# Layer 1's routing: experts chosen from logits in two parts, ranks summed by TensorE into one bank, two-byte columns with the tile innermost, gather ids first

## The reference, cut to what matters

```
logits = xf @ Wg                                  # (4096, 8)
probs = softmax(logits, axis=-1)
vals, idx = top_k(probs, 2)
w = vals / (sum(vals, axis=-1, keepdims=True) + 1e-09)
counts = zeros(8); combine = zeros((4096, 8))
for k in range(2):
    oh = one_hot(idx[:, k], 8)
    pos = cumsum(oh, axis=0) - 1 + counts[None, :]    # rank in the expert's queue
    keep = (oh == 1) & (pos < 256)
    counts = counts + sum(keep, axis=0)
    combine = combine + w[:, k][:, None] * keep
out = sum over e of combine[:, e] * (gelu(xf @ W1[e] + b1[e]) @ W2[e] + b2[e])
```

## Time and profile before

| | us |
|---|---|
| median of 3 runs | 897.94 |
| lowest, highest | 897.37, 899.93 |
| the profiled execution, its own time | 897.85 |
| the profiled execution, its span | 895.6 |

### The profile page before, as it was taken

One profiled execution on the slowest core, in us unless ns is written; L12 is line 12 of the kernel. 1 busy time (PEld: TensorE's weight loads), 2 busy tenths in 40 slices (PEclk: granted clock), 3 DMA queues, 4 the chain that ended last, 5 costly groups with the idle time before them and its releaser, 6 DMA issues.

```text
span 895.6 us, 33689 instructions
## 1 busy us (share of the span) xinstructions
PE 713.8 (80%) x14638; PEld 644.2 (72%) x14639; DVE 658.0 (73%) x1076; ACT 491.7 (55%) x724; POOL 558.3 (62%) x412
## 2 busy tenths in 40 slices
PE   4467636882688999999999999999999988915846
PEld 2137425771677999899989899988988887904846
DVE  3788553453587999999999999999998989284104
ACT  5465302342474677578668667757676656554310
POOL 4011046524257989988999988888878888404630
PEclk9677658996699999999999999999999999855978
DMA  7731142331006000000000000000000000420137
GB/s 192 242 79 48 49 90 58 71 64 54 21 5 193 6 10 7 6 7 10 7 6 10 18 4 4 15 4 3 4 15 4 4 15 16 149 100 26 46 105 200
DMA packets 67595, 44.01 MB, mean 49 GB/s; under 512 B 22000, under 2 KB 62208, under 8 KB 67328
## 3 DMA queue, kind: packets, MB, share of 16 engines
q1 hardware_dynamic: 64128, 35.11, 13.8%
q0 software_dynamic: 3328, 6.82, 3.3%
HBM read 27.76 MB, written 14.16 MB: 47 GB/s over the span
## 4 chain that ended last, share of the span: by engine, by line
PE 67%; DVE 10%; issue 9%; ACT 7%; another core or an unknown queue 3%; DMA 2%; SPq 2%; POOL 1%; DVEq 0%; POOLq 0%; ACTq 0%
PE psum L1811 16%; PE psum L1911 6%; PE psum L1866 6%; PE psum L1844 6%; PE psum L1902 4%; PE psum L1873 3%; PE psum L1859 3%; PE psum L1881 3%; PE psum L1745 2%; ACT arena L1007 2%; PE psum L2120 2%; PE psum L1760 2%; PE psum L1852 2%; PE psum L1620 1%
## 5 line engine op out<-in xcount | busy, mean ns | idle before, releaser
L1811 PE MATMUL psum<-hT,w_qkv 128*128 128x128 f32 x1408 | 173.9, 281 | 2.0 <-DVE arena L1363 1.6
L1811 PEld LDWEIGHTS psum<-hT,w_qkv 128*128 128x128 f32 x1408 | 164.5, 194 | 5.2 <-DVE arena L1363 1.8
L563 POOL TENSOR_TENSOR arena<-arena,small 128x1024 f32<-128x1024 f32 x56 | 106.0, 1914 | 56.1 <-DVE small L1376 56.1
L542 POOL TENSOR_TENSOR arena<-arena 128x1024 f32<-128x1024 f32 x56 | 106.7, 1905 | 12.6 <-ACT arena L890 11.4
L528 POOL TENSOR_TENSOR arena<-arena 128x1024 f32<-128x1024 f32 x56 | 106.5, 1902 | 0.0
L1369 DVE TENSOR_REDUCE small<-arena 128x16 f32<-128x1024 f32 x60 | 73.1, 1219 | 8.8 <-ACT arena L879 6.6
L518 POOL DMA_INDIRECT arena<-h_rows,route x40 | 40.2, 1004 | 58.1 <-issue 43.2
L567 POOL TENSOR_TENSOR arena<-arena 128x1024 f32<-128x1024 f32 x28 | 65.9, 2353 | 16.3 <-DVE arena L1396 16.2
L1357 DVE TENSOR_REDUCE small<-psum 128x16 f32<-128x1024 f32 x60 | 72.8, 1215 | 2.6 <-PE psum L1911 2.6
L1363 DVE TENSOR_TENSOR arena<-psum,small 128x1024 f32<-128x1024 f32 x60 | 70.5, 1215 | 0.1
L1844 PE MATMUL psum<-arena 64*128 64x64 f32 x1344 | 62.4, 231 | 10.0 <-issue 7.4
(11 more groups left out here) (319 smaller groups left out, 1643.7 us busy)
## 6 DMA issues: line engine op xcount, KB each, us to landing
y_rows<-hT SPq DMA_DIRECT2D x8, 512.0 KB, 6.6
arena<-y_rows SPq DMA_DIRECT2D x8, 512.0 KB, 6.0
o_rows<-arena SPq DMA_DIRECT2D x10, 256.0 KB
x_sb<-in_L_attn_u SPq DMA_DIRECT2D x8, 256.0 KB, 4.6
arena<-in_W_inT SPq DMA_DIRECT2D x16, 128.0 KB
arena<-in_W_out SPq DMA_DIRECT2D x64, 32.0 KB
h_rows<-arena SPq DMA_DIRECT2D x4, 512.0 KB, 3.3
h_rows<-hT SPq DMA_DIRECT2D x8, 256.0 KB, 2.3
```

What stands on the lines that cost most here:

```text
L542: pool.tensor_tensor(x3, x3, lr[:, tile_of(t) * 32 + k * H:tile_of(t) * 32 + k * H + H].unsqueeze(2).to_broadcast([P, H, D]), ALU.mult).th ...
L563: pool.tensor_tensor(z4, z4, r3.unsqueeze(3).to_broadcast([P, 8, 2, CH]), ALU.mult).then_inc(done, 1)
L1811: mm = pe.matmul(ps[bank][:, p * P:(p + 1) * P], w_qkv[:, j * HD + p * P:j * HD + (p + 1) * P], hT[:, at:at + P], start=True, stop=True)
```

## The change

All of it lies in steps 1 to 7 above.

- The logits of chunks 0 to 5 get a signal of their own. PE now does the logits of chunks 4 and 5 before it turns chunk 6, those of chunk 6 before it turns chunk 7. The second part goes to another bank. Tiles are numbered chunk by chunk.
- DVE chooses the experts by the logits minus their maximum, read straight from PSUM, in eleven operations: once for chunks 0 to 5 (192 elements) and once for chunks 6 and 7 (64). One-hot columns are written as bf16 with expert and choice outermost and the tile innermost. After each part it adds up the columns from chunk to chunk (`sum_up`, eight operations of 64 elements).
- ACT's exponential stands aside from the choice; a second small one gives the second value relative to the first, and the weights come from these.
- PE forms complete ranks in one bank: columns ahead in the tile, running sums of the chunk before, and full sums of the batch pairs before (in the line with `all_ones` and the one with `first_half`), besides the expert totals in four matmuls of 8 columns.
- DVE multiplies, caps, adds and reduces that to the rank, in five operations; the two products of number and slot half are between bf16 operands with the tile innermost.
- The gather's ids are made in five operations right after PE's result; the scatter's follow.
- POOL makes one more mask and one more table at the start.

```diff
+        masks = sb("masks", [P, 5 * P], BF16)
+        pair_no = sb("pair_no", [P, 2 * T], BF16)
...
+            chain.link(pool.memset(first_half[CH:P, :], 0.0))
+            chain.link(pool.memset(first_half[0:CH, 0:CH], 0.0))
+            chain.link(pool.iota(pair_no[:, :], pattern=[[T, 2], [1, NC], [NC, BP]], base=1, channel_multiplier=0, **imprecise))
...
-            act.activation(pr1, sh1, ACT.Exp).then_inc(ex_done, 1)
+            act.activation(pr1, sh1, ACT.Exp)
+            act.activation(tile_f, tile_f, ACT.Exp).then_inc(ex_done, 1)
...
+            def choose(lg, c0, c1):
+                ...
+                chain.link(dve.tensor_reduce(per(mx), part(lg), AX_X, ALU.max))
+                chain.link(dve.tensor_tensor(part(sh1), part(lg), wide(mx), ALU.subtract))
+                chain.link(dve.scalar_tensor_tensor(part(pick1), part(sh1), 0.0, order, ALU.is_equal, ALU.mult))
+                chain.link(dve.tensor_reduce(per(m2), part(pick1), AX_X, ALU.max))
+                chain.link(dve.tensor_tensor(hot(0), part(pick1), wide(m2), ALU.is_equal))
+                chain.link(dve.scalar_tensor_tensor(part(sh2), hot(0), -1e30, part(sh1), ALU.mult, ALU.add))
+                chain.link(dve.tensor_reduce(per(tile_f), part(sh2), AX_X, ALU.max))
+                chain.link(dve.tensor_tensor(part(sh2), part(sh2), wide(tile_f), ALU.is_equal))
+                chain.link(dve.tensor_tensor(part(sh2), part(sh2), order, ALU.mult))
+                chain.link(dve.tensor_reduce(per(m2), part(sh2), AX_X, ALU.max))
+                return dve.tensor_tensor(hot(1), part(sh2), wide(m2), ALU.is_equal)
...
+            dve.wait_ge(lg_mm, 2)
+            chain.link(choose(ps[1][:, L:L + T * E], 0, NC - 2))
+            for c in range(NC - 3):
+                chain.link(sum_up(c))
+            sum_up(NC - 3).then_inc(rhs_ready, 1)
+            dve.wait_ge(rhs_ready, 3)
+            dve.wait_ge(lg_mm, 3)
+            choose(ps[0][:, 0:T * E], NC - 2, NC).then_inc(oh_done, 1)
+            dve.wait_ge(oh_done, 2)
+            chain.link(sum_up(NC - 2))
+            sum_up(NC - 1).then_inc(rhs_ready, 1)
+            dve.tensor_tensor(et(numbers[:, 0:512]), et(oh1), over_e2(pair_no[:, :], E), ALU.mult)
+            chain.link(dve.tensor_scalar(numbers[:, 512:1024], oh1, part_no, None, ALU.mult))
             dve.wait_ge(ex_done, 2)
             chain.link(dve.tensor_reduce(e_sum, te(pr1), AX_X, ALU.add))
+            chain.link(dve.scalar_tensor_tensor(row_f, e_sum, 1e-9, tile_f, ALU.mult, ALU.add))
+            chain.link(dve.tensor_scalar(row_f, row_f, 1.0, None, ALU.add))
+            chain.link(dve.reciprocal(wk[:, 0:T], row_f))
+            dve.tensor_tensor(wk[:, T:2 * T], wk[:, 0:T], tile_f, ALU.mult).then_inc(wk_set, 1)
             dve.wait_ge(cnt_done, 2)
+            dve.tensor_tensor(k3(scr1)[:, :, 0, :], k3(ranks)[:, :, 0, :], k3(oh1)[:, :, 0, :], ALU.mult)
+            chain.link(dve.tensor_scalar(cap1, total, float(CAP), None, ALU.min))
+            chain.link(dve.tensor_tensor(r3, k3(ranks)[:, :, 1, :], cap1.unsqueeze(2).to_broadcast([P, E, T]), ALU.add))
+            chain.link(dve.tensor_tensor(k3(scr1)[:, :, 1, :], r3, k3(oh1)[:, :, 1, :], ALU.mult))
+            chain.link(dve.tensor_reduce(pos, scr1.rearrange("p (e t) -> p t e", e=E), AX_X, ALU.add))
+            dve.tensor_scalar(first, pos, float(P), None, ALU.is_lt)
+            chain.link(dve.tensor_scalar(beyond, pos, float(P), None, ALU.is_ge))
+            dve.scalar_tensor_tensor(rows_b[:, :], beyond, -float(P), pos, ALU.mult, ALU.add)
+            chain.link(dve.scalar_tensor_tensor(second, pos, float(CAP), beyond, ALU.is_lt, ALU.mult))
+            for j, tile in enumerate((first, second)):
+                last = dve.tensor_tensor(r4[:, j], numbers..., over_e2(tile, 2 * E), ALU.mult)
...
+            chain.link(dve.tensor_copy(in3, found[:, :, E:2 * E]))
+            chain.link(dve.scalar_tensor_tensor(row3, found[:, :, 0:E], float(P), in3, ALU.mult, ALU.add))
             chain.link(dve.tensor_scalar(in3, row3, -float(P), 0.0, ALU.add, ALU.max))
             chain.link(dve.tensor_scalar(off3, in3, float(B * L), -float(B * L), ALU.is_ge, ALU.mult))
+            dve.tensor_tensor(ids_i[:, 0:2 * E]..., in3, off3, ALU.add).then_inc(ids_set, 1)
...
-            for c in range(3, NC):
+            for c in range(3, NC - 2):
                 second_turn(c)
                 second_logits(c - 2)
+            second_logits(NC - 4)
+            second_logits(NC - 3).then_inc(lg_mm, 1)
+            second_turn(NC - 2)
             second_logits(NC - 2)
+            second_turn(NC - 1)
             second_logits(NC - 1).then_inc(lg_mm, 1)
...
+            def ahead_in_tile(c0, c1):
+                pe.matmul(tiles_of(ranks, c0, c1), before_own, tiles_of(oh1, c0, c1), start=(c0 == 0), stop=False)
+            def ahead_in_batch(c0, c1):
+                pe.matmul(tiles_of(ranks, c0, c1), own_ones, tiles_of(up_to, c0 - 1, c1 - 1), start=False, stop=False)
             pe.wait_ge(rhs_ready, 3)
+            ahead_in_tile(0, NC - 2)
+            ahead_in_batch(1, NC - 2)
             pe.wait_ge(rhs_ready, 4)
+            ahead_in_tile(NC - 2, NC)
+            ahead_in_batch(NC - 2, NC)
+            for b in range(BP - 1):
+                pe.matmul(r4[:, :, :, b + 1:BP], all_ones, sums[:, :, b:b + 1].unsqueeze(2).to_broadcast([P, 2 * E, NC, BP - 1 - b]),
+                          start=False, stop=False)
+            pe.matmul(r4, first_half, sums.unsqueeze(2).to_broadcast([P, 2 * E, NC, BP]), start=False, stop=True)
+            for b in range(BP):
+                mm = pe.matmul(ps[2][:, 512:512 + E], all_ones, first_sums[:, :, b], start=(b == 0), stop=(b == BP - 1))
+            mm.then_inc(cnt_done, 1)
+            pe.wait_ge(rhs_ready, 5)
...
-                mm = pe.matmul(ps[0][:, 0:32], hot_of(pos_hot, t), rhs1[:, t * 32:(t + 1) * 32],
+                mm = pe.matmul(ps[0][:, 0:32], hot_of(pos_hot, t), rhs1.rearrange("p (r t) -> p r t", t=2 * T)[:, :, t],
```

More of the change, by code:

```diff
@@ L1508, in _ @@
-            dve.tensor_copy(ohb1, oh1).then_inc(rhs_ready, 1)
-            chain.link(dve.tensor_tensor(row_f, top[0], top[1], ALU.add))
-            chain.link(dve.tensor_scalar(row_f, row_f, 1e-9, None, ALU.add))
-            chain.link(dve.reciprocal(row_f, row_f))
-            for k in range(2):
-                last = dve.tensor_tensor(wk[:, k * T:(k + 1) * T], top[k], row_f, ALU.mult)
-            last.then_inc(wk_set, 1)
-            dve.wait_ge(cnt_done, 2)
-            own, both, pref = ps[3][:, 512:1024], ps[2][:, 0:512], ps[3][:, 0:512]
@@ L1556, in _ @@
             last.then_inc(rhs_ready, 1)
-            chain.link(dve.tensor_copy(rows_b[:, :], row1))
             for n in range(2 * T // 8):
```

121 lines of the change are left out of this document (41 added, 80 removed).

## The result

| | before | changed |
|---|---|---|
| median of 20 runs each, us | 902.98 | 894.68 |
| lowest, highest | 896.90, 908.24 | 889.97, 901.11 |
| the profiled execution, its own time | 897.85 | 894.4 |
| its span | 895.6 | 892.6 |

The ratio is 0.9904 [0.9881, 0.9926]: faster, but by 8.3 us where 12.2 were forecast (0.9864).

A forecast was written before the change was run, and what follows sets the result against it. The prediction took the serial routing, 30.9 us of small DVE operations from 784.50 to 815.36, as the bound. Its terms brought the ids to 803.15, a gain of 12.2: 897.85 - 12.2 = 885.7 us, range 883.0 to 889.0.

The forecast's parts named there:

- Logits in two parts: PE's logits ahead of routing: second signal at 786.4 against 784.50, a price of 1.9 us for two bare ACT copies.
- Choice, part one: DVE's choice over 192 elements, from 779.7 to 785.5 beside PE, ending 0.9 before the second logits.
- Ranks and numbers: PE's rank matmuls give counts at 791.45; DVE's numbers 0.33 + 0.30, weights signalled 791.9; later two one-hot products, 1.25 together.
- Ids: DVE's five operations of 16 ahead of the gather: 1.05 us, ids at 803.15 where before 815.36.
- The diagonal matrices: ACT's 64 matrices, needed by the first expert product's end at 813.1, end at 810.7: cover 2.4, where it was 12.3.
- the constants: POOL's wider mask, two memsets and table at the start: some 0.85, hidden beside PE's DMA wait until 9.31, so nothing.
- A: Narrow PSUM runs slow the rank matmuls: at four times the column price 887.1, with dearer number products 887.9; chance 0.10.
- B: Scattered reads of 32 columns make PE the bound of the id stage: at twice the pitch 890.5; chance 0.07.
- E: Slower: the id matmuls' scattered reads so dear that the gain is lost, 901.4 at 10 ns a column; chance 0.04.
- C: ACT's diagonal matrices become the bound and gelu waits: 887.8 at a slip of 4.5; chance 0.03.
- D: Expert stage falls into another rhythm; PE's 2.34 idle ahead of the seventh expert vanishes or recurs: 883.3 or 888; chance 0.06.
- The rule on memory lines: Weighed against PE's new operands: access to other 16-byte SBUF lines costs, non-contiguous PSUM access slows matmuls; no figure given.

The follow-up runs named there:

- delay: Changed kernel with six additional DVE operations of 512 elements between PE's id product and DVE's id operations; 898.06 us, ratio 0.9915 to the kernel before.
- hot_t: Changed kernel with the two writes of the one-hot columns walked with the tile innermost, so contiguous; 895.28 us, ratio 0.9884 to the kernel before.
- consts_only: Kernel before with only the change's wider mask, table and what fills them, later tensors 384 bytes further; 873.04 us, ratio 1.0018 to the kernel before.
- tail: Changed kernel with its added mask and table allocated behind everything else, one memset more; 857.74 us, ratio 0.9842 to the kernel before.
- after_c: Changed kernel repeated unchanged, in the set with 871.61 for the kernel before; 862.38 us, ratio 0.9889.
- before_again: Kernel before repeated unchanged for a second profile; 875.55 us, ratio 0.9997 to itself.
- before_c: Kernel before, unchanged, a single execution for a profile in the set where its median was 906.31; 907.49 us.
- pad512: Changed kernel with 128 unused bytes ahead of `iota_b`, so later tensors begin 512 bytes further instead of 384; 888.06 us, ratio 0.9869 to the kernel before.
- best_tail: Changed kernel with contiguous one-hot writes, first part ending at chunk 4, and added mask and table allocated last; 858.80 us, ratio 0.9836 to the kernel before.

## Why the prediction was wrong

**What bounds the kernel**: right. The routing is serial and what it gains moves all behind it: *delay* moved the end of the routing by 4.0 and left the length behind as it was; both kernels in one set have 83.8 and 84.0 there. This rests on the traces, as the medians of *delay* leave 2.5 of the 4.35.

**The sum of the routing**: right to half a microsecond. Four traces of before have 44.8, 45.5, 46.6 and 46.1, mean 45.7; four of the changed kernel 34.8, 34.0, 33.6 and 33.3, mean 33.9. That is 11.8 for the 12.2 of the sum. Inside it terms err both ways:

- *Logits in two parts.* Forecast 1.9 later. From the turn of chunk 2, before needs 13.9 to 15.7, mean 14.9; changed 17.8, 17.0, 16.6 and 16.3, mean 16.9: 2.0. In the changed trace chunk 3's logits too ran at the half clock: three chunks in a row took 5.13 and the first signal came at 784.4, 10.8 behind the turn, where the working has 9.1 (779.7). The waits for ACT's copies are there, 0.69 each.
- *Choice, part one.* It was to end 0.9 before the second logits. It ended 791.48, and PE 791.38: the cover was just used up. The fault is in two operations, 1.01 each where 0.39 had been taken from the f32 rows, as the one-hot columns are written 128 bytes apart. *hot_t* halves them. In part two they cost 0.44 for 0.27.
- *Ranks and numbers.* The recorded terms for PE's counts add up to 791.40, not 791.45; DVE is the later either way. Numbers 0.33 + 0.38 for 0.33 + 0.30, the products 1.29 for 1.25. The sum of 512 reads with a stride and takes 1.02 for 0.69.
- *Ids.* 1.01 for 1.05, read 0.78 behind PE.
- *The diagonal matrices* end 2.3 ahead of the first gelu's table load, for the 2.4 of the cover.

**The step that failed**: the constants. The prediction had them "at the start ... nothing" and priced POOL's time alone, 0.85 beside a wait that ends at 9.31. POOL's time did cost nothing: its last constant ends at 8.92 and PE starts at 9.32, still behind the DMA. But a constant also takes room, and this one stood ahead of the working memory. The change shows one gain, 11.8, and a loss in parts of the kernel it does not touch: 0.9 in S, from the last store, and 0.6 ahead of the final sum, from the loads. Together they are 1.5, and *consts_only* against its before has 1.4 [-0.5, 3.7].

The gap of the forecast was 3.9 (12.2 for 8.3). The routing has 0.4 of it and the constants 1.5; the other 2.0 stay open. They are no more than the measurement leaves: the interval of the ratio means a gain of 6.7 to 10.7, and 11.8 - 1.5 is 10.3. *tail* against *after_c* gives 4.6, more than the 1.5 that the traces show, so the size of what the constants cost is known only as 1 to 5 us. Their sign and place are shown by S, the last store and the loads.

One candidate for the rest is the start of layer 1's attention. In the lower sets its first 64 projection matmuls take 24.4 to 26.0 in the four traces with the tensors 384 bytes later and 23.1 in the four others. The difference is the clock, here in *before_again* and *consts_only*, with the window of the second row (us, busy PE, PEld, DVE, ACT, POOL, PEclk, DMA share, GB/s):

```profile
224.11 2.05 PE L1811 MATMUL psum<-hT,w_qkv 128*128 128x128 f32 x16 [1.87 <-DVE arena L1363]
```

```profile
225.85 3.68 PE L1815 MATMUL psum<-hT,w_qkv 128*128 128x128 f32 x16 [1.88 <-DVE arena L1367]
226.00:229.40 3.40, 3.40 (x16) 3.24 (x16) 3.27 (x3) 1.62 (x2) 0.00 (x0) 0.50 0.00 0
```

The granted clock is 2.4 GHz in the first and 1.2 GHz in the window. In the four microseconds ahead PE was busy for 2.13 of them in either, at 2.4 GHz, so the rows do not say why it fell in one. Nor does the loss show further on: from the first projection to the turn of chunk 2 *consts_only* needs 541.0, less than the 541.7 to 543.9 of the four with the tensors in their old place.

In the first pair the stretch began 3.0 late. From the first projection to that turn both traces have 548.4, so all of it lies ahead: 0.9 in S, and 2.1 in layer 0 ahead of it, where *before* and *before_c*, the same kernel, differ by 1.6 too.

With the constants out of the way the forecast holds: 12.2 of 897.85 is a ratio of 0.9864; *tail* has 0.9842 and 0.9847, *pad512* 0.9869. That it comes so near, and beyond for *tail*, is in part luck, as the routing's 11.8 alone is 0.9869.

**The rivals.** A was true in a small way: 384, 256 and 128 columns in runs of 3, 2 and 1 took 0.85 (795.49 to 796.34), 1.1 ns a column for 0.81, hidden beside DVE. B and E are refuted: 64 matmuls reading 32 columns 128 bytes apart take 4.81, for 4.80. DVE's comparisons still set that pace, so what the reads cost is only known to be covered by 75 ns a matmul. C did not come about. D's wait came, but not by the shift of 12 us: *before_c* has it too. ACT and DVE start long after PE's recorded ends, here ahead of the seventh expert of the changed kernel, where the matmuls that feed ACT's first row end at 836.76:

```profile
842.25 1.56 ACT L1020 ACTIVATE arena<-psum,arena 128x256 f32<-128x256 f32 x4 [7.12 <-remote]
...
844.38 0.42 DVE L1570 COPY arena<-psum 128x256 f32<-128x256 f32 x1 [4.62 <-remote]
844.86 3.06 PEld L2107 LDWEIGHTS psum<-arena 128*128 128x128 f32 x8 [6.29 <-issue]
844.86 3.78 PE L2107 MATMUL psum<-arena 128*128 128x256 f32 x8 [6.10 <-issue]
```

PE's gap of 6.1, for 2.34 before, is nearly all of the 84.2 against 80.3 of the first pair. In the sets near 875 the gap is absent. Its cause stays open.

**The rule on memory lines** that was weighed against the change (the Trainium skill, "Advanced Engine Details and Errata", section "Memory Cachelines"): its SBUF half shows in DVE's writes, 1.01 against 0.50, and not in PE's reads, as far as the pace of 75 ns tells; its PSUM half shows in 1.1 against 0.81 ns a column.

**A version that beats both**: *tail*, 857.74 beside 862.38 and 871.61, and *best_tail*, 858.80, which can't be told from it. Against the changed kernel the intervals still overlap a little.

## What to carry to other kernels

When a change adds a tensor, ask what lies behind it in SBUF and by how many bytes it is pushed; put new constants behind the working memory, or keep the old places, and look at transfers far from the change for a common shift. A transfer that has become a tenth of a microsecond slower can lose nine tenths when another one waits behind it. One trace of before and one of after can differ by 4 us in a stretch that nothing touched, so check a stretch against a second trace of each before explaining it. Two-byte results should be written with the innermost index contiguous even where the reader wants another order.

## What the runs showed of the hardware

- With the tensors in SBUF 384 bytes later, a 256 KB store lands after 2.28 to 2.30 instead of 2.17 to 2.18 us and 512 KB loads after 7.2 to 7.3 instead of 5.9 to 6.5; at 512 bytes later, 2.18 and 6.4.
- One 8 KB packet on the instruction queue, served ahead of a store's last packet instead of behind it, moved the store's landing from 2.44 to 2.46 us to 3.35 to 3.38; where it was served behind, with the tensors still 384 bytes later, it was 2.63.
- DVE writes 192 two-byte elements 128 bytes apart in 1.01 us (5.3 ns each), 0.50 with the tile innermost; a sum over 512 with a stride takes 1.02 instead of 0.69.
- The same kernel has medians 23 to 35 us apart between sets of runs, with ratios between kernels nearly alike; of the upper ones' surplus some 14 us lie ahead of layer 1's first projection, 6 to 9 in the start of the attention and some 8 behind the ids.
